# Local attention in a hybrid block: division before the transposes, transposed value product, split q and k transposes, Ln and Exp for the lengths, band by TensorE

## The reference, cut to what matters

```python
q = l2norm(q) * qs; k = l2norm(k) * ksc            # 8 heads of 64
q, k = rotary_xpos(q, k)
# windows of 64 queries see their own and the previous window of keys
sim = einsum('bhwid,bhwjd->bhwij', bq, bk)
sim = where(mask, -max, sim)
attn = softmax(sim, axis=-1)
out = einsum('bhwij,bhwjd->bhwid', attn, bv)
x = x + out @ wo
```

## Time and profile before

| | us |
|---|---|
| median of 3 runs | 2242.17 |
| lowest and highest | 2241.56, 2242.24 |
| the profiled execution's own time | 2243.29 |
| its span, first to last instruction | 2241.4 |

### The profile page before, as it was taken

How to read it: one execution, slowest core, us unless ns; L and a number is a source line. 1 busy time by engine, 2 the same in 40 slices (tenths; PEclk the granted TensorE clock), 3 DMA queues, 4 the chain that set the end, 5 groups by cost and what they waited for, 6 DMA issues and landing times.

```text
span 2241.4 us, 53938 instructions
## 1 busy us (share of the span) xinstructions
PE 2125.9 (95%) x19264; PEld 1468.6 (66%) x19264; DVE 1683.1 (75%) x4031; ACT 1541.9 (69%) x4254; POOL 1680.3 (75%) x1712
## 2 busy tenths in 40 slices
PE   6999879999899999899999999999999989999988
PEld 4777557777567777556666656666777756777765
DVE  6777568888568888677677777777888856888865
ACT  3666358888548998626656656657888954889862
POOL 6778779998258888448877787868999834888852
PEclk9999889999999999999999999999999999999999
DMA  4000001112111112121211121111111211111211
GB/s 118 1 1 1 7 21 44 26 41 49 44 32 36 38 39 50 46 67 46 57 46 41 51 58 42 52 27 23 36 32 44 46 45 30 33 38 40 47 31 51
DMA packets 121369, 88.38 MB, mean 39 GB/s; under 512 B 85560, under 2 KB 102160, under 8 KB 118800
## 3 DMA queue, kind: packets, MB, share of 16 engines
q1 hardware_dynamic: 118544, 82.69, 15.3%
q10 hardware_dynamic: 2560, 2.24, 0.4%
HBM read 30.38 MB, written 8.39 MB: 17 GB/s over the span
## 4 chain that ended last, share of the span: by engine, by line
PE 43%; DVE 16%; POOL 14%; issue 5%; SPq 5%; DMA 2%; ACT 1%; POOLq 0%; DVEq 0%
PE bank L1351 11%; POOL store L1163 8%; POOL store L1172 6%; PE bank L1362 5%; PE bank L600 5%; PE bank L1342 5%; DVE store L986 4%; SPq L473 4%; DVE store L991 3%; DVE store L998 3%; PE bank L639 3%; PE bank L730 2%; PE bank L652 2%; PE bank L678 2%; PE bank L614 2%
## 5 line engine op out<-in xcount | busy, mean ns | idle before, releaser
L1575 POOL TENSOR_SCALAR store<-store 128x512 f32<-128x512 f32 x512 | 349.8, 697 | 107.9 <-DVE store L1502 105.9
L1502 DVE CUSTOM_DVE_ANT_0 store<-bank,store 128x512 f32<-128x512 f32 x512 | 335.6, 688 | 120.2 <-PE bank L1342 67.3
L1458 ACT ACTIVATE store<-bank 128x512 f32<-128x512 f32 x512 | 286.8, 600 | 201.5 <-PE bank L1351 198.1
L854 ACT ACTIVATE store<-bank,store 128x128 f32<-128x128 f32 x1024 | 363.4, 375 | 47.9 <-DVE store L1004 47.8
L1163 POOL TENSOR_TENSOR store<-store 128x16 f32<-128x16 f32 x128 | 372.7, 2912 | 27.7 <-DVE store L1000 27.2
L1157 POOL TENSOR_TENSOR store<-store 128x512 f32<-128x512 f32 x256 | 321.2, 1277 | 94.3 <-DVE store L991 90.9
L1351 PEld LDWEIGHTS bank<-store 128*128 128x128 f32 x2048 | 240.1, 142 | 133.5 <-ACT store L1458 75.8
L1351 PE MATMUL bank<-store 128*128 128x128 f32 x2048 | 298.4, 277 | 0.0
L1172 POOL TENSOR_TENSOR store<-store 128x512 f32<-128x512 f32 x256 | 261.7, 1044 | 10.0
L600 PE MATMUL bank<-store 128*128 128x512 f32 x496 | 253.1, 596 | 0.0
L1004 DVE TENSOR_REDUCE store<-bank 128x4 f32<-128x512 f32 x256 | 164.8, 686 | 89.8 <-PE bank L639 89.5
(11 more groups left out here) (224 smaller groups left out, 4556.2 us busy)
## 6 DMA issues: line engine op xcount, KB each, us to landing
store<-store SPq DMA_DIRECT2D x256, 128.0 KB, 2.4
store<-parts SPq DMA_DIRECT2D x96, 192.0 KB
parts<-store SPq DMA_DIRECT2D x16, 384.0 KB, 3.7
store<-store SPq DMA_DIRECT2D x128, 32.0 KB
store<-store SPq DMA_DIRECT2D x128, 31.8 KB
store<-store SPq DMA_DIRECT2D x32, 127.0 KB
store<-in_L_ffn_wqkv_dram SPq DMA_DIRECT2D x4, 768.0 KB, 4.5
out_dram<-store SPq DMA_DIRECT2D x8, 256.0 KB, 2.4
```

Of the source, the lines that this page charges most:

```text
L854: last = nc.scalar.activation(prob[:, e, b, :], bank[3 + e][:, b * P:(b + 1) * P], ACT.Exp, bias=nmax[:, e, b:b + 1], accum_out=psums[:, h ...
L1458: nc.scalar.activation(AT[:, h % 4, c, :], bank[SCORE_BANKS + (64 * q + 4 * h + c) % TURN_BANKS][:, :], ACT.Exp, scale=-1.0).then_inc(aexp ...
L1502: nc.vector.tensor_tensor_reduce(out=S[:, h % 4, t, :], in0=bank[(64 * q + 4 * h + t) % SCORE_BANKS][:, :], in1=decay[:, off:off + L], sca ...
L1575: nc.gpsimd.tensor_scalar(s_, s_, -1.0, amax[:, h % 4, t:t + 1], ALU.mult, ALU.add).then_inc(shifted_done, 1)
```

## The change

It does six things.

1. **Division ahead of the transposes.** `take_o`, `o_transpose` and `onorm` are gone. The row sums are inverted separately for each half `e`, and the probabilities themselves are multiplied by the inverse in place: half 0 on GpSimd, half 1 on VectorE, each a 128x512 product with both inputs in on-chip memory (SBUF).
2. **The product with the values is made transposed.** The value block is the fixed operand and the transposed probabilities stream, so the output leaves TensorE with features on partitions, as `project_out` needs it.
3. **q's and k's transposes stand apart**, one before and one behind the product with the values.
4. **Ln and Exp for the lengths**: GpSimd's power is replaced by two ScalarE activations on 128x16, at the end of ScalarE's list for the tile; the clip on VectorE becomes a maximum of two tensors. The activation table with both functions is loaded by name before. In the written order no table load stands between the activations of the attention's loop.
5. **The band by TensorE** in every tile, so that the two band writes and their waits go.
6. **A stage later**: the second half of the probabilities is transposed behind the scores of the next tile, and `project_out` works on the tile before the last. ScalarE's order becomes: squares, exponentials 0, copy of half 1 of the tile before, exponentials 1, output, q and k, v, copy of half 0, Ln, Exp.

```diff
+        def inverse_lengths(act, q, j):
+            flat = norm[:, 2 * (j % 2):2 * (j % 2) + 2, :].rearrange("p i h -> p (i h)")
+            act.wait_ge(clip_done, 4 * q + j + 1)
+            nc.scalar.activation(flat, flat, ACT.Ln).then_inc(log_done, 1)
+            act.wait_ge(log_done, 4 * q + j + 1)
+            nc.scalar.activation(flat, flat, ACT.Exp, scale=-0.5).then_inc(norm_done, 1)
...
-                for e in range(0 if written else 2):
+                for e in range(2):
...
-                pe.wait_ge(exp_done, n2 + e + 3)
+                pe.wait_ge(scaled_p[e], 4 * q + j + 1)
...
-                            last = nc.tensor.matmul(bank[7][half * WIN:(half + 1) * WIN, h * DH:(h + 1) * DH],
-                                                    probT[:, e, b, half * WIN:(half + 1) * WIN], v[:, j, h * DH:(h + 1) * DH],
+                            last = nc.tensor.matmul(bank[7][e * DH:(e + 1) * DH, b * P + half * WIN:b * P + (half + 1) * WIN],
+                                                    v[:, j, h * DH:(h + 1) * DH], probT[:, e, b, half * WIN:(half + 1) * WIN],
                                                     start=True, stop=True, skip_group_check=True)
...
-            def o_transpose(q, j):
...
-                nc.vector.tensor_scalar(flat, flat, 1e-24, None, ALU.max).then_inc(clip_done, 1)
+                nc.vector.tensor_tensor(flat, flat, least[:, :], ALU.max).then_inc(clip_done, 1)
...
+            def inverse_sums(q, j, e):
+                dve.wait_ge(exp_done, 8 * q + 2 * j + e + 3)
+                nc.vector.reciprocal(pinv[:, e, :], psums[:, e, :]).then_inc(pinv_done[e], 1)
+
+            def scale_probs(q, j, e):
+                dve.wait_ge(pinv_done[e], 4 * q + j + 1)
+                nc.vector.tensor_tensor(prob[:, e, :, :], prob[:, e, :, :], bc(pinv[:, e, :], 2, P), ALU.mult).then_inc(scaled_p[e], 1)
...
-                nc.gpsimd.tensor_tensor(flat, flat, minus_half[:, 0:2 * H], ALU.pow).then_inc(norm_done, 1)
+            def scale_probs(q, j):
+                pool.wait_ge(pinv_done[0], 4 * q + j + 1)
+                nc.gpsimd.tensor_tensor(prob[:, 0, :, :], prob[:, 0, :, :], bc(pinv[:, 0, :], 2, P), ALU.mult).then_inc(scaled_p[0], 1)
```

More of the change, by code:

```diff
@@ L608, in project_v, with qk_transpose_one, scores @@
                                  start=True, stop=True).then_inc(v_done, 1)
[L610 to L617 removed]
+            def qk_transpose_one(q, j, i):
+                pe.wait_ge(roped_done, 8 * q + 2 * j + i + 5)
+                for b in range(PAIRS):
+                    last = nc.tensor.transpose(bank[5 + i][:, b * P:(b + 1) * P], roped[:, i, b * P:(b + 1) * P], ident)
+                last.then_inc(qkT_done, 1)
+            def qk_transpose(q, j):
+                qk_transpose_one(q, j, 0)
+                qk_transpose_one(q, j, 1)
+            def scores(q, j, ff_ahead=False):
                 n2 = 8 * q + 2 * j
@@ L688, in attention_sequence @@
                     has_next, has_ahead = more or j < 3, more or j == 0
-                    scores(q, j, has_prev, ff_ahead and j == 0)
+                    scores(q, j, ff_ahead and j == 0)
                     if has_prev:
-                        weigh_values(*prev)
+                        prob_transpose(*prev, 1, True)
+                    if has_prev2:
+                        project_out(*prev2)
                     if more or j < 2:
@@ L873, in attention_sequence @@
                 for j in range(TPS):
+                    prev, has_prev = (q, j - 1) if j else (q - 1, TPS - 1), before or j > 0
                     if more or j < 2:
@@ L1033, in attention_sequence @@
                         ff_normalize(ff_from, 0, ff_from == 0)
-                    has_prev = before or j > 0
-                    prev = (q, j - 1) if j else (q - 1, TPS - 1)
                     if j and more:
@@ L1178, in finish_qk, with attention_sequence @@
                 add_turned(q, j, 1)
-                inverse_norms(q, j)
                 normalize(q, j, 0)
                 normalize(q, j, 1)
-            def attention_sequence(s, q, more, norm_more=False):
+            def attention_sequence(s, q, more, norm_more=False, ff_from=None):
                 for j in range(TPS):
+                    if ff_from is not None and j == 3:
+                        ff_rstd(ff_from, 0)
+                    scale_probs(q, j)
                     if more or j < 2:
@@ L1212, in transformer_pool @@
                 for s in range(B):
[L1213 to L1214 removed]
+                    attention_sequence(s, q0 + s, s < B - 1, l == 0 and s < B - 2, q0 if s == B - 1 else None)
                 ff_rstd(q0 + 1, 1)
```

135 lines of the change are left out of this document (53 added, 82 removed).

## The result

The changed kernel takes **2202.82 us** (median of 4 runs, 2200.31 to 2203.65), the kernel before 2242.2 (4 runs, 2241.56 to 2242.31): a ratio of 0.9823, 95% interval 0.9806 to 0.984. That is 39.4 us faster; the forecast was 31 us, as 2211 in a range of 2192 to 2240. The profiled execution took 2203.05, its span is 2201.3.

A forecast was written before the change was run, and what follows sets the result against it. TensorE's work, 7.98 of an 8.22 us period, plus waits for GpSimd bound the kernel. Layers -33.0, layer ends +2.4, call starts -0.5 each: -31.6 from 2243.3 is 2211.7; the median 1.1 lower, 2211, range 2192 to 2240.

The forecast's parts named there:

- the new ring: Plain tile: band, maxima, exponentials, ScalarE's copy, values, then TensorE's list back to the band; period 8.11 us.
- The step that lets the values wait for ScalarE's copy: Plain tile: ScalarE's copy of half 1 ends 4.10 after the band; TensorE, there at 3.84, waits to start the values.
- Nothing else in the plain tile is later: Plain tile: the lists of ScalarE, VectorE and GpSimd all fit within the 8.11 us period; ScalarE's slack 0.19.
- rival 4: TensorE's own work binds, copy of half 1 in time: period 7.72 to 7.95, 27 us less, 2184; chance 0.08.
- The 0.13 for a restart in the new ring: At the values: a TensorE stall ends with some 0.13 us more, added between 4.10 and 3.88 in the period.
- Ln and Exp: ScalarE, end of its tile list: the pair replaces GpSimd's power (2.91) and takes 0.36 us, as in the mixer.
- The ports in layer 0: VectorE's two-SBUF-input instructions wait for GpSimd in layer 0's 24 norm tiles: 0.2 us a tile charged, bounds 0 and 1.2.
- Rival 1: Layer 0: norm work pushes VectorE's product behind GpSimd's multiplication in every second norm tile: +19 us, 2230; chance 0.20.
- Rival 3: All tiles: the product of half 1 regularly loses to GpSimd's multiplications; slower than before, about 2290; chance 0.08.
- The last tiles of a layer: Last sequence, without the two projections: distances of the maxima 7.9, 7.4 and 7.1 us.
- ScalarE's own ring of 6.9: Last sequence: ScalarE's list of copies and exponentials takes over as the bound at 6.9 us, against 6.4 without the projections.
- The start of the first call: Start of each call: GpSimd's power (2.91) leaves, Ln and Exp wait for ScalarE: -0.5 us, bounds 0 and -2.5.

The follow-up runs named there:

- add_first: The changed kernel with VectorE's addition of the projected output moved ahead of the rotation of q: 2205.9 us, ratio 0.984.
- before_lnexp: The kernel before with ScalarE's logarithm and exponential in place of GpSimd's power, nothing else of the change: 2212.3 us, ratio 0.9869.
- both_first: The changed kernel with ScalarE's copy of half 1 ahead of exponentials 0 and VectorE's output addition ahead of q's rotation: 2200.96 us, ratio 0.9815.
- no_clip: The changed kernel without VectorE's clip, ScalarE's logarithm taking x + 1e-24 through its bias: 2198.66 us, ratio 0.9803.
- copy_no_clip: The changed kernel with ScalarE's copy of half 1 ahead of exponentials 0 and VectorE's clip taken out: 2179.37 us, ratio 0.9723.
- pow_back: The changed kernel with the power back on GpSimd in place of ScalarE's logarithm and exponential: 2318.31 us, ratio 1.0345.
- copy_first: The changed kernel with ScalarE's copy of half 1 of the tile before moved ahead of the exponentials of half 0: 2182.3 us, ratio 0.9743.

## Why the prediction was right, and where it was wrong

**Direction, size and the new ring: right, in part by luck.** Period 8.11 forecast, 8.12 measured; the pieces 4.23 and 3.88 came as 4.19 and 3.93. The step that lets the values wait for ScalarE's copy was true, as *add_first* shows: with the addition out of the way, the period does not move. "Nothing else in the plain tile is later" held too, but by 0.03 us only, and without having been looked at for this wait. VectorE's list had been added up in the text (1.32 to the maxima and 1.20 + 1.20 + 0.27 behind them, 3.99), and the addition never set beside the values that wait for it (4.10). It cost no accuracy here, and would have cost the next step: moving the copy gives 0.12 a tile, not 0.19.

**TensorE's floor (rival 4): mis-sized.** "The work is 7.98 of a period of 8.22; the two stalls cost 0.11 and 0.13." They are no waits for another engine. *before_lnexp* waits for nobody and still takes 8.23. Against the prediction's pieces its chain has 0.19 more in the v projection behind the values' products (1.05 instead of 0.86), 0.15 more in half 0's transposes behind the output's (0.59 instead of 0.44), and 0.09 less in the last ones with x's. So the floor went from 8.23 to 7.93. The difference, 0.30, is near the forecast's 0.26; the level was 0.21 too low. TensorE therefore comes to the values at 4.00 behind the band (*both_first*), not at 3.84, and waits for 0.19, not for 0.39. The 0.13 for a restart in the new ring, taken from those two, thus had no basis; that 0.15 lies between the copy's end and the values' start (445.56 to 445.71) made the term come out all the same, and that is luck.

**Ln and Exp: right.** GpSimd's busy time fell by 246.8 (239 forecast), the pair takes 0.36 to the start of what follows (450.13 to the squares at 450.49), as in the earlier trace rows. The slack behind it was smaller than forecast. The prediction's own terms (-0.16, 0.49, 0.36 and 1.08) add up to 1.77, not to 1.85; the squares end 1.93 behind the band and the exponentials start at 2.06, so 0.13 is left, not 0.19. The Trainium skill ("ScalarE: Activation LUTs", the decision table's row on a tight latency budget), with its about 0.3 for each activation, would have given an estimate of 0.63 for the two; the trace differs, 0.21 for each and 0.24 from one start to the next.

**The ports in layer 0: 0.2 charged, 0 measured.** The means are 8.10 a tile in layer 0 and 8.07 in layer 1, and the difference is all in the first distance (7.89 against 7.12). The blocking is there: the clip is blocked in plain tiles (median 1.28 over all), and in one tile in four with norm work (12 in all) the product of half 1 is in its place:

```profile
456.42 1.63 DVE L1012 TENSOR_TENSOR store<-store 128x512 f32<-128x512 f32 x1
457.97 0.59 DVE L969 TENSOR_SCALAR store<-store 128x128 f32<-128x128 f32 x2
...
459.09 1.29 DVE L1003 TENSOR_REDUCE store<-bank 128x4 f32<-128x512 f32 x2 [0.34 <-PE bank L640]
```

Even there the maxima wait 0.34 for TensorE, so VectorE was not late; and the norm's pair is over at 458.56, when GpSimd's multiplications start at 458.79. Rival 1 was a real mechanism with a threshold that the kernel stays under, by 0.23 here; *both_first* crosses it, by making the rest faster. Rival 3's, the product of half 1 behind GpSimd's multiplications, is in no trace; where its cause is shown above, the product is held up by the additions.

**The last tiles of a layer: mis-sized.** Forecast 7.9, 7.4, 7.1; measured 8.41, 8.38, 7.13, so 1.5 more a layer, and 7.0 in all, since the last one is 8.04 in layer 0 of the second call. The step took TensorE's missing projections and ScalarE's own ring of 6.9, and forgot that in these tiles VectorE also computes statistics for the feed-forward part. VectorE, from one maxima to the next:

```profile
878.63 1.25 DVE L1003 TENSOR_REDUCE store<-bank 128x4 f32<-128x512 f32 x2
...
885.71 0.86 DVE L1052 BATCH_NORM_STATS2 store<-store 128x6 f32<-128x128 f32 x4
...
887.01 1.26 DVE L1003 TENSOR_REDUCE store<-bank 128x4 f32<-128x512 f32 x2
```

No row of VectorE in between has idle time, so these 8.38 are all its own list, and the clip's blocking (1.24 at 883.74) is in it. Without the clip (*no_clip*, *copy_no_clip*) the two distances are 8.09 to 8.14. The forecast's four stretches add up to 1004.7, measured are 1003.6. That is so near by luck: 9.6 charged for the ports and not paid, against 7.0 more in the last tiles, 0.4 more in the first distances and 1.0 more from 0.01 a plain tile.

**The start of the first call: -0.5 forecast, -6.0 measured.** This is most of the 8 us by which the change beat its forecast, and most of it is not the term's mechanism. The same additions on GpSimd, before and now:

```profile
298.20 2.48 POOL L1157 TENSOR_TENSOR store<-store 128x512 f32<-128x512 f32 x2
```

```profile
294.03 2.49 POOL L1145 TENSOR_TENSOR store<-store 128x512 f32<-128x512 f32 x2
```

So 4.2 of the 6.0 are there before the power's turn, in the end of the mixer; up to 263 us the two traces are within 0.1 of each other. Of the 4.2, 1.5 are GpSimd's making of the band table, one cast now where there were three (lines 423 and 425 of before, 0.61 each, and their waits), which the prediction did not count. In the rest TensorE has the same products at different clocks: between 271.6 and 281.8 the granted clock was 0.50 of 2.4 GHz before and 0.83 now. What can belong to the power's leaving is the stretch from these additions to the first maxima, 12.81 before and 11.02 now, so 1.8 (10.65 in *before_lnexp*, so 2.2), and that is inside the prediction's bound of -2.5.

## What to carry to other kernels

Before pricing a ring, write beside each of its waits the second latest thing it waits for; where two end close together, moving one alone gives only the difference between the starts that each would allow (here 0.12, for ends 0.03 apart). An engine's floor is best read from a stretch where nothing waits, since a gap between starts can be the engine's own cost. And an exclusive conflict between two engines is worth nothing or a great deal depending on the slack around it, so after each speed-up it has to be priced again: here taking the same clip out was worth 0.6 us in a stretch of layer 0 (251.05 against 250.42), and 13 us once both waits were gone (257.01 against 244.04), though in both cases VectorE's product only took over the clip's place beside GpSimd.

## What the runs showed of the hardware that was not expected

- **TensorE, a piece that costs more by what stands ahead of it.** Four 128x128 transposes take 0.59 behind weights of 64 columns and 0.44 behind a projection. Two 128x512 projections for v take 1.05 instead of 0.86; the four for q and k 1.91 instead of 1.72. That the narrow weights are the cause is not shown: in *before_lnexp* the four transposes of half 0 take the same 0.59 behind the output's transposes, which have 128 columns. What both have in common in the trace is that the first weight load starts with the products (446.79 and 446.79 for k's transposes), where it starts 0.42 ahead of them in the case of 0.44 (448.58 and 449.00).
- **VectorE beside GpSimd.** A 128x16 maximum of two SBUF operands takes 0.2 us alone, and 1.24 to 1.29 when it meets one of GpSimd's 128x512 additions. The 128x512 product takes 0.69 alone and 1.62 to 1.72 when it meets one. An instruction with a single SBUF tensor and per-partition scalars was held up too: line 969 took 2.07 for the pair in *both_first*, started 0.15 behind GpSimd's multiplications, and 0.59 where they had not begun. The power on GpSimd took 2.91 on average before, and 3.24 in *pow_back*.
- **The clock in an unchanged stretch.** Ahead of the local attention the changed kernel and *copy_first* have the same instructions. The columns are the stretch, busy time of PE, PEld, DVE, ACT and POOL, granted clock, DMA share, GB/s; the first row is the changed kernel, the second *copy_first*.

```profile
0.00:263.00 263.00, 224.25 (x1266) 170.85 (x1282) 192.94 (x464) 144.32 (x311) 200.51 (x324) 0.96 0.10 27
```

```profile
0.00:263.00 263.00, 224.19 (x1290) 170.29 (x1306) 194.41 (x467) 145.95 (x317) 205.41 (x333) 0.99 0.10 27
```

The granted clock was 0.96 and 0.99 of 2.4 GHz, and GpSimd's instruction of line 2130 that starts at 262.48 in the one starts at 257.50 in the other. The first maxima came at 305.05 and at 299.08. So 6 us of a difference between two single executions can come from this part, 5 of them ahead of 263 us, and *copy_first*'s own runs spread over 12 us. What sets the clock there was not tried.
